# Two graph convolutions: rows as three bfloat16 parts, one-hots made by ScalarE, ring of 16 slots

## What is computed

```python
def _gcn_conv(x, src, dst, W, b):
    deg_out = jnp.maximum(jax.ops.segment_sum(ones, src, num_segments=N), 1.0)
    deg_in = jnp.maximum(jax.ops.segment_sum(ones, dst, num_segments=N), 1.0)
    h = x * (deg_out ** (-0.5))[:, None]
    h = h @ W
    m = jax.ops.segment_sum(h[src], dst, num_segments=N)
    return m * (deg_in ** (-0.5))[:, None] + b

h = _gcn_conv(layernorm(x), src, dst, W1, b1)
h = jax.nn.relu(h)
h = _gcn_conv(h, src, dst, W2, b2)
x = x + _layer_norm(h, gamma, beta)
```

## Time and profile before

| | us |
|---|---|
| median of three runs | 5920.07 |
| profiled execution, its own time | 5863.58 |
| span of the profiled execution | 5861.9 |
| TensorE busy (of the span) | 3845.1 |
| VectorE busy | 2575.1 |
| ScalarE busy | 966.5 |
| GpSimd busy | 2943.7 |
| mean granted TensorE clock | 0.793 |

### The profile page before, as it was taken

The page is one execution under the profiler, slowest core; times in us unless marked ns, Lnnn a source line. Parts: engine busy times, 40 slices in busy tenths (PEclk is TensorE's granted clock), DMA queues, the critical chain, the costliest instruction groups (busy, mean ns, idle before and its releaser), DMA issues.

```text
span 5861.9 us, 62152 instructions
## 1 busy us (share of the span) xinstructions
PE 3845.1 (66%) x14313; PEld 2804.7 (48%) x14313; DVE 2575.1 (44%) x7839; ACT 966.5 (16%) x2299; POOL 2943.7 (50%) x2860
## 2 busy tenths in 40 slices
PE   1666667777788799999355555554655555556368
PEld 0333335566667588888233333333433333334257
DVE  8433234555576511111244444445444444445841
ACT  5333232222102522222200000000200000000421
POOL 0666665565300033333366666667266666664513
PEclk9777778888898799999667767666767776767669
DMA  2333335565687344444433333332233333332202
GB/s 78 106 105 108 105 106 178 185 195 186 198 254 235 107 109 115 111 109 110 140 88 93 91 92 92 92 92 80 81 91 92 92 92 92 92 92 84 88 16 32
DMA packets 322621, 660.17 MB, mean 113 GB/s; under 512 B 60683, under 2 KB 142923, under 8 KB 322150
## 3 DMA queue, kind: packets, MB, share of 16 engines
q0 software_dynamic: 148960, 365.25, 21.4%
q1 hardware_dynamic: 152870, 253.42, 14.4%
q10 hardware_dynamic: 20448, 37.52, 2.1%
HBM read 488.94 MB, written 174.87 MB: 113 GB/s over the span
## 4 chain that ended last, share of the span: by engine, by line
PE 20%; issue 11%; DVE 10%; another core or an unknown queue 6%; DVEq 2%; DMA 1%; ACT 1%; SPq 0%; POOL 0%; POOLq 0%; ACTq 0%
PE bank L1769 15%; DVE reg_b L1313 6%; DVEq L304 2%; PE bank L1717 2%; DVE reg_a L1298 1%; PE bank L1728 1%; PE bank L1689 1%; DVEq L1313 1%; DVE small L822 0%; DVE work L1471 0%; DMA conv_rows<-work 0%; PE bank L1750 0%; DVE work L1505 0%; ACT reg_b L681 0%
## 5 line engine op out<-in xcount | busy, mean ns | idle before, releaser
L1769 PE MATMUL bank<-work,reg_a 128*128 x3520 | 1329.6, 526 | 1175.0 <-issue 626.0
L617 POOL DMA_INDIRECT work<-conv_rows,tables x1662 | 1575.8, 948 | 935.5 <-issue 482.9
L1769 PEld LDWEIGHTS bank<-work,reg_a 128*128 128x128 f32 x3520 | 821.3, 256 | 1683.2 <-issue 1570.1
L1313 DVE TENSOR_TENSOR reg_b<-reg_b,bank 128x257 f32 x1760 | 743.1, 422 | 1026.2 <-remote 518.6
L578 POOL DMA_INDIRECT messages<-work,small x880 | 884.3, 1005 | 536.3 <-ACT work L708 251.2
L1628 PE MATMUL bank<-reg_b,reg_a 128*128 x1760 | 602.8, 477 | 427.6 <-issue 191.1
L1298 DVE TENSOR_SCALAR reg_a<-iota,tables 128x128 f32<-128x128 f32 x1760 | 553.7, 315 | 274.9 <-issue 197.5
L1628 PEld LDWEIGHTS bank<-reg_b,reg_a 128*128 128x128 f32 x1760 | 363.1, 229 | 610.1 <-issue 569.8
L708 ACT ACTIVATE work<-bank,tables 128x256 f32<-128x256 f32 x880 | 397.7, 474 | 1042.5 <-PE bank L1628 630.4
L599 POOL DMA_INDIRECT residual_rows<-work,slot_t x112 | 177.9, 1589 | 478.2 <-DVE work L1282 308.3
L1641 PE MATMUL bank<-reg_b,reg_a 128*128 128x257 f32 x1544 | 395.0, 405 | 28.3 <-DVE reg_a L1164 16.3
(11 more groups left out here) (340 smaller groups left out, 3827.5 us busy)
## 6 DMA issues: line engine op xcount, KB each, us to landing
reg_b<-messages SPq DMA_DIRECT2D x316, 258.0 KB
reg_a<-in_L_ffn_W_dram SPq DMA_DIRECT2D x56, 1024.0 KB, 5.4
reg_a<-item_rows SPq DMA_DIRECT2D x110, 256.0 KB
work<-conv_rows,tables POOLq DMA_INDIRECT x1662
b_rows<-messages ACTq DMA_DIRECT2D x72, 258.0 KB
reg_b<-messages ACTq DMA_DIRECT2D x70, 258.0 KB
b_rows<-messages SPq DMA_DIRECT2D x56, 258.0 KB
messages<-work,small POOLq DMA_INDIRECT x880
```

What stands on the lines that cost most here:

```text
L617: g.indirect_dma_start(GC[:, u, 0:D], None, table, bass.IndirectOffsetOnAxis(ap=BSRC[:, b_:b_ + 1], axis=0)).then_inc(z(f"conv_in{u // 4}" ...
L1313: v.tensor_tensor(acc, acc, ps[i % 8][:, 0:D + 1], ALU.add).then_inc(z(f"{tag}_add"), 1)
L1769: pe.matmul(ps[i % 8][:, 0:D + 1], OHP[:, i % (2 * OHN), :], GCf[:, bass.ds(offs[i % 4], D + 1)], start=True, stop=True).then_inc(z(f"{tag ...
```

## The change

Each row of the tables is stored as three bfloat16 parts, head, middle and rest, whose sum is the fp32 row exactly: 768 bfloat16 values, 1536 bytes. The head is the upper half of the fp32 word; the first rest is the difference; its upper half is the middle; the second difference is the rest. ScalarE copies heads and middles, VectorE makes the two differences, chunk by chunk, in the `ln3` stage and in `c1`; the stages now write fp32 rows into a staging buffer XF (in `reg_a`) and the parts into XR.

A slot of the ring has 770 bfloat16 values, and the ring 16 slots in place of 24. TensorE makes three bfloat16 matmuls per item into the same PSUM bank with the same one-hot, the smallest part first; the column of ones stands beside the rests.

The one-hots are made by ScalarE in bfloat16, four items at a time: |iota - destination| by four Abs activations (128x128), then relu(1 - that) over 128x512, into a ring of 20 one-hots. VectorE only adds.

SyncE keeps both relays, landings and releases, in one loop (`relays`), the landings three groups ahead. The semaphores of both convolutions are shared (`conv_oh`, `conv_add`, `conv_dist`), and their counts go on from p1 to p2. The table of slot offsets is computed for the new slot count and size.

The core of the diff:

```diff
@@ setup
-    UM = UC = 24
+    UM, UC = 24, 16
-        conv1_t = dram("conv1_rows", [T * P, D])
-        conv2_t = dram("conv2_rows", [T * P, D])
+        conv1_t = dram("conv1_rows", [T * P, 3 * D], BF16)
+        conv2_t = dram("conv2_rows", [T * P, 3 * D], BF16)
-        OHN = 4
-        OHP = ta[:, 0:2 * OHN * P].rearrange("p (s n) -> p s n", n=P)
+        OHR = 20
+        OHP = ta[:, 0:OHR * P // 2].bitcast(BF16).rearrange("p (s n) -> p s n", n=P)
+        DIST = ta[:, OHR * P:(OHR + 8) * P].rearrange("p (s n) -> p s n", n=P)
-        GCf = work[:, 0:UC * (D + 1)]
-        GC = GCf.rearrange("p (u w) -> p u w", w=D + 1)
+        GCf = work[:, 0:UC * SLOT // 2].bitcast(BF16)
+        GC = GCf.rearrange("p (u w) -> p u w", w=SLOT)
+        XR = XR.bitcast(BF16).rearrange("p (s t d) -> p s t d", s=2, d=PARTS)
+        XF = ta[:, 0:2 * CH * D].rearrange("p (s t d) -> p s t d", s=2, d=D)
+        XFH = ta[:, 0:2 * CH * D].bitcast(BF16).rearrange("p (s t d k) -> p s t d k", s=2, d=D, k=2)[:, :, :, :, 1]
+        XL = B2B[:, 0:CH * D].rearrange("p (t d) -> p t d", d=D)
+        XLH = B2B[:, 0:CH * D].bitcast(BF16).rearrange("p (t d k) -> p t d k", d=D, k=2)[:, :, :, 1]
@@ SyncE
-                sp.wait_ge(*norms("ln3", "norm", c + 1))
+                for part in ("head", "middle", "rest"):
+                    sp.wait_ge(z(f"part_{part}"), PARTED["p1"] + c + 1)
                 sp.dma_start(nodes(conv1_t, c), XR[:, c % 2, :, :]).then_inc(z(f"rows_out{c % 2}"), 16)
-            def arrivals(tag):
-                for k in range(NB4):
-                    sp.wait_ge(z(f"conv_in{k % (UC // 4)}"), gathered(tag, k))
-                    sp.sem_inc(z(f"{tag}_landed"), min(4, NBLK - 4 * k))
-            arrivals("p1")
+            def arrived(tag, k):
+                sp.wait_ge(z(f"conv_in{k % (UC // 4)}"), gathered(tag, k))
+                sp.sem_inc(z(f"{tag}_landed"), min(4, NBLK - 4 * k))
+            def relays(tag):
+                for k in range(AHEAD):
+                    arrived(tag, k)
+                for k in range(NB4 - AHEAD):
+                    if k < NB4 - UC // 4:
+                        sp.wait_ge(z(f"{tag}_mm"), sp.value_load(ROW_L[:, k:k + 1], min_val=1, max_val=NI))
+                        sp.sem_inc(z(f"{tag}_free"), 4)
+                    arrived(tag, k + AHEAD)
+            relays("p1")
-                sp.wait_ge(z("relu1"), (c + 1) * CH)
+                for part in ("head", "middle", "rest"):
+                    sp.wait_ge(z(f"part_{part}"), PARTED["p2"] + c + 1)
                 sp.dma_start(nodes(conv2_t, c), XR[:, c % 2, :, :]).then_inc(z(f"rows_out{c % 2}"), 16)
-            arrivals("p2")
-            sp.wait_ge(z("p2_add"), NI)
+            relays("p2")
@@ GpSimd
-                    g.indirect_dma_start(GC[:, u, 0:D], None, table,
+                    g.indirect_dma_start(GC[:, u, 0:PARTS], None, table,
@@ ScalarE
+            def heads(tag, c):
+                if c >= 2:
+                    act.wait_ge(*parts_free(tag, c))
+                a.copy(XR[:, c % 2, :, 0:D], XFH[:, c % 2]).then_inc(z("part_head"), 1)
+            def middles(tag, c):
+                act.wait_ge(z("part_left"), PARTED[tag] + c + 1)
+                a.copy(XR[:, c % 2, :, D:2 * D], XLH).then_inc(z("part_middle"), 1)
             for c in range(NCH + 1):
                 if c < NCH:
                     ln_std("ln3", c)
                 if c >= 1:
                     if c >= 3:
-                        act.wait_ge(*rows_out((c - 1) % 2, 1, (c - 1) // 2))
-                    ln_apply("ln3", c - 1, lambda i: X[:, (c - 1) * CH + i, :], lambda i: XR[:, (c - 1) % 2, i, :])
-            def releases(tag):
-                for k in range(0, NB4 - UC // 4):
-                    act.wait_ge(z(f"{tag}_mm"), act.value_load(ROW_L[:, k:k + 1], min_val=1, max_val=NI))
-                    act.sem_inc(z(f"{tag}_free"), 4)
-            releases("p1")
+                        act.wait_ge(z("part_left"), c - 2)
+                    ln_apply("ln3", c - 1, lambda i: X[:, (c - 1) * CH + i, :], lambda i: XF[:, (c - 1) % 2, i, :])
+                    act.wait_ge(*norms("ln3", "norm", c))
+                    heads("p1", c - 1)
+                if c >= 2:
+                    middles("p1", c - 2)
+            middles("p1", NCH - 1)
+            def target_hots(tag):
+                def distances(i):
+                    if i >= 8:
+                        act.wait_ge(z("conv_oh"), CONV[tag] * NI + i - 4)
+                    for k in range(i, i + 4):
+                        ins = a.activation(DIST[:, k % 8, :], IOTA[:], ACT.Abs, bias=DREL[:, k:k + 1], scale=-1.0)
+                    ins.then_inc(z("conv_dist"), 4)
+                act.wait_ge(z("conv_ready"), CONV[tag] + 1)
+                distances(0)
+                for i in range(0, NI, 4):
+                    if i + 4 < NI:
+                        distances(i + 4)
+                    act.wait_ge(z("conv_dist"), CONV[tag] * NI + i + 4)
+                    if i >= OHR:
+                        act.wait_ge(z(f"{tag}_mm"), i - OHR + 4)
+                    a.activation(OHP[:, i % OHR:i % OHR + 4, :], DIST[:, i % 8:i % 8 + 4, :], ACT.Relu, scale=-1.0,
+                                 bias=ONES[:, 0:1]).then_inc(z("conv_oh"), 4)
+            target_hots("p1")
...
+                if c >= 1 and t % CH == 0:
+                    act.wait_ge(z("relu1"), c * CH)
+                    heads("p2", c - 1)
+                if c >= 1 and t % CH == 4:
+                    middles("p2", c - 1)
+            act.wait_ge(z("relu1"), T)
+            heads("p2", NCH - 1)
+            middles("p2", NCH - 1)
+            target_hots("p2")
@@ VectorE
-                def onehot(i):
-                    if i >= 8:
-                        v.wait_ge(z(f"{tag}_mm"), i - 7)
-                    v.tensor_scalar(OHP[:, i % 8, :], IOTA[:], DREL[:, i:i + 1], None, ALU.is_equal
-                                    ).then_inc(z(f"{tag}_oh"), 1)
-                v.memset(GC[:, :, D:D + 1], 1.0).then_inc(z(f"{tag}_one"), 1)
-                for i in range(OHN):
-                    onehot(i)
+                v.memset(GC[:, :, PARTS:PARTS + 1], 1.0).then_inc(z("conv_one"), 1)
                 for i in range(NI):
                     if i % 4 == 0:
                         offs = table_offsets(DVE_, ROW_D[:, i:i + 4], (T - 1) * (D + 1))
-                    if i + OHN < NI:
-                        onehot(i + OHN)
                     v.wait_ge(z(f"{tag}_mm"), i + 1)
                     if i:
-                        v.wait_ge(z(f"{tag}_add"), i)
+                        v.wait_ge(z("conv_add"), CONV[tag] * NI + i)
                     acc = ACCf[:, bass.ds(offs[i % 4], D + 1)]
-                    v.tensor_tensor(acc, acc, ps[i % 8][:, 0:D + 1], ALU.add).then_inc(z(f"{tag}_add"), 1)
+                    v.tensor_tensor(acc, acc, ps[i % 8][:, 0:D + 1], ALU.add).then_inc(z("conv_add"), 1)
...
+            def rests(tag, c):
+                n = PARTED[tag] + c
+                if n:
+                    v.wait_ge(z("part_middle"), n)
+                    v.wait_ge(z("part_rest"), n)
+                v.tensor_tensor(XL, XF[:, c % 2], XFH[:, c % 2], ALU.subtract).then_inc(z("part_left"), 1)
+                v.wait_ge(z("part_left"), n + 1)
+                if c >= 2:
+                    v.wait_ge(*parts_free(tag, c))
+                v.tensor_tensor(XR[:, c % 2, :, 2 * D:PARTS], XL, XLH, ALU.subtract).then_inc(z("part_rest"), 1)
+            for c in range(NCH + 2):
                 if c < NCH:
                     v.wait_ge(z(f"x_in{c}"), 16 * (2 + (c == NCH - 1)))
                     ln_stats("ln3", c, lambda i: X[:, c * CH + i, :])
-                if c >= 1:
+                if 1 <= c <= NCH:
                     ln_scale("ln3", c - 1, extra=DO)
+                if c >= 2:
+                    v.wait_ge(*norms("ln3", "norm", c - 1))
+                    rests("p1", c - 2)
...
+                c = t // CH - 1
+                if c >= 0 and t % CH == 2:
+                    v.wait_ge(z("relu1"), (c + 1) * CH)
+                    rests("p2", c)
+            v.wait_ge(z("relu1"), T)
+            rests("p2", NCH - 1)
@@ TensorE
-                            table_offsets(PE_, ROW_C[:, i:i + 4], (UC - 1) * (D + 1)))
+                            table_offsets(PE_, ROW_C[:, i:i + 4], (UC - 1) * SLOT))
                 after = places(0)
                 for i in range(NI):
                     if i % 4 == 0:
...
                         pe.wait_ge(z(f"{tag}_landed"), need)
                     if i % 4 == 1 and i + 3 < NI:
                         after = places(i + 3)
-                    pe.wait_ge(z(f"{tag}_oh"), i + 1)
+                    pe.wait_ge(z("conv_oh"), CONV[tag] * NI + i + 1)
                     if i >= 8:
-                        pe.wait_ge(z(f"{tag}_add"), i - 7)
-                    pe.matmul(ps[i % 8][:, 0:D + 1], OHP[:, i % (2 * OHN), :], GCf[:, bass.ds(offs[i % 4], D + 1)],
```

(30 more changed lines are left out.)

17 lines of the change are left out of this document (11 added, 6 removed).

## The result

The changed kernel takes 6022.3 us (median; 6020.1 to 6025.0) against 5919.9 (5917.0 to 5927.4): ratio 1.0177, interval 1.016 to 1.0194, 102 us slower. The forecast was 5969, 49 slower. The sign and the range held; the forecast was less than half of the measured size.

A forecast was written before the change was run, and what follows sets the result against it. No engine is full; POOL's pauses over its 1.2525 us per gather, from cycles with a slow half, bound the convolutions. Loops +28, edges +20, +29, -22, -6 give +49: 5863.6 + 49 + 56.5 = 5969 us, range 5625 to 6190.

The forecast's parts named there:

- The loops: Gather loops of both convolutions: slightly slower pace of TensorE and VectorE, +14 us each, +28 for two (0 to +120).
- the balance: Formula for POOL's streak in a loop cycle, pause 3.2 us, fast half 10.5 us: rate 1.417 to 1.434 us a gather.
- f: Time per item in the fast half of a loop cycle: 0.75 us before, 0.80 taken for the change.
- s: Time per item in the slow half of a loop cycle: 3.1 us before, 3.3 taken, 4.1 as bound.
- S: Gathers in one POOL streak between pauses, by formula: 19.5 before, 17.6 taken for the change.
- Before conv1: Splitting rows in the statistics stage: VectorE becomes the pace at 8.3 us per chunk, +20 us (10 to 35).
- Before conv2: Splitting rows in the linear stage: 3 us per chunk, 21, plus 8 after the last Relu, +29 us (8 to 62).
- End of conv1: No VectorE one-hot held beside POOL's pass over X, -22 us (-24 to 0); fewer items left, -3.
- B: Rival for the loops: slow halves vanish, POOL streams at its floor, 5639 us; chance 0.28 with its partial form.
- A: The forecast itself: pause cycle stays, edges cost, a gather every 1.43 to 1.46 us, 5969 us; chance 0.41.
- C: Rival for the loops: TensorE's item sets the pace, streaks of 8 to 12, +86 per convolution, 6113 us; chance 0.24.
- D: Rival for the loops: pauses follow bytes or packets, which grow by half, +76 per convolution, 6093 us; chance 0.05.

The follow-up runs named there:

- before_again: The kernel before, unaltered, run for a second profile where POOL never pauses: 5301.7 us.
- after_short_rows: Changed kernel with tables and gathers of two of three parts (1024 bytes), still three matmuls, where POOL never pauses: 5355.9 us, ratio 1.0102.
- fp32_act_hots: Kernel before with one-hots on ScalarE and relays on SyncE, fp32 rows and ring of 24 kept, where POOL never pauses: 5293.4 us, ratio 0.9985.
- the second set: Runs where POOL pauses, kernel before at 5915.3 us: changed kernel unaltered 6020.0; kernel before with a ring of 16, 5904.3.
- the fifth: Set where POOL pauses, kernel before at 5877.4 us: changed kernel with two-part tables 5979.6, unaltered 5983.4; kernel before with ring of 16, 5861.5.
- narrow_fp32: Kernel before with ScalarE's one-hots, SyncE's relays and ring of 16, its fp32 product cut to 96 of 257 columns: 5855.4 us beside 5868.0.
- fp32_act_hots_c: Kernel before with ScalarE's one-hots and SyncE's relays, fp32 and ring of 24, rerun where POOL pauses: 5852.2 us, ratio 0.9963.

## Why the prediction was right or wrong

**What bounds the kernel** was read rightly: pauses of POOL over a floor of 1.2525, in cycles with a slow stretch. In the changed kernel such a stretch looks so:

```profile
3388.00 0.42 DVE L1372 TENSOR_TENSOR reg_b<-reg_b,bank 128x257 f32 x1 [0.20 <-DVE reg_b L1372]
...
3390.60 0.42 DVE L1372 TENSOR_TENSOR reg_b<-reg_b,bank 128x257 f32 x1 [2.18 <-PE bank L1851]
...
3393.36 0.35 PE L1851 MATMUL bank<-work,reg_a 128*128 x1 [0.43 <-issue]
...
3394.15 0.42 DVE L1372 TENSOR_TENSOR reg_b<-reg_b,bank 128x257 f32 x1 [3.12 <-PE bank L1851]
...
3395.95 0.42 DVE L1372 TENSOR_TENSOR reg_b<-reg_b,bank 128x257 f32 x1 [0.20 <-DVE reg_b L1372]
```

Adds mostly 0.62 us apart until 3388.0, then 2.6 and 3.6 us apart, then 0.62 again; PE's matmuls single between.

The prediction says that no view names what slows PE. The trace does show it, in the rows of PE's sequencer (PEldq), which don't count as busy. Below is its register step ahead of the product (count: ns min/median/max), in this order: the fast half of the cycle of the earlier trace rows, the slow half, the slow stretch above in the changed kernel, and before_again, where POOL never pauses:

```profile
L1769 PEldq FUSED_REGOPS  x11: 37/37/37, 3397.1 to 3405.6; - x11
...
L1769 PEldq FUSED_REGOPS  x5: 10/685/700, 3407.5 to 3419.3; - x5
...
L1851 PEldq FUSED_REGOPS  x6: 3/695/700, 3388.3 to 3394.0; - x6
...
L1769 PEldq FUSED_REGOPS  x420: 37/37/37, 3000.9 to 3498.9; - x140
```

The same step takes 37 ns in one half and some 700 in the other. PE's sequencer has 330 and 300 steps of 0.60 to 0.76 us in the two convolutions of before, 391 and 390 in those of after, 2 and 3 in before_again and none in after_short_rows. VectorE's sequencer has none in before and after: there VectorE waits for PE. Why a step takes 0.7 us stays open. The sets show that it belongs to where the kernel runs and not to the kernel (two chips without pauses, three others with; the two chips that came twice kept their kind, though one of them had before at 5915 and at 5873): the same program has it or not, the message stage with it (1394 to 1438 us with pauses, 1155 to 1160 without). I had taken the pause as a property of the loop.

**POOL's cost per gather, SyncE's relays, ScalarE's one-hots, the shorter ring at 0**: right. 945 ns with 1536 bytes; relays 5300.8 against 5301.0; 0.50 us an item where 0.69 was the bound; ring of 16 at 1.436. The rule of the Trainium skill ("ScalarE: Activation LUTs", Rules for kernel authors) to use VectorE for simple functions agrees with the trace in direction: a one-hot costs 0.50 us on ScalarE against 0.315 on VectorE. The kernel is none the slower for it (fp32_act_hots: 0.9985), since neither engine sets the end.

**The loops: the step that failed.** +14 each was taken; +28 was measured in the second set (1230.5 and 1230.1 us against 1202.9 and 1201.5), +30 in the fifth (1224.5 and 1220.8 against 1193.0 and 1192.1), 42 between the first two profiles. The step that failed is the balance: it kept the fast half of a cycle at 10.5 us and the pause at 3.2, and let the change act on the pace alone (f 0.80 for 0.75, s 3.3 for 3.1). The adds of the two profiles show what happened. Call a stretch fast where at least five adds in a row start within 1.6 us of the one before, and the rest slow; both convolutions together:

| | before | after |
|---|---|---|
| fast stretches: mean length, us an item | 10.5, 0.81 | 6.2, 0.84 |
| slow stretches: mean length, us an item | 11.6, 3.8 | 7.4, 3.3 |
| items in fast and in slow stretches | 1391, 326 | 1333, 398 |
| time in fast and in slow stretches, us | 1124, 1236 | 1114, 1329 |

f moved little, as taken. s fell, where a rise was taken. What changed is the length of a fast stretch, 6.2 us in place of 10.5, and with it the number of items that fall into slow ones. The whole loss of the loops stands in slow stretches, and other limits than 1.6 us (1.4, 2.0) show the same. The bound f = 0.94, s = 4.1 gave 1.49, near the 1.486 of the profile, but with S = 13.5 and values of f and s that didn't come: that it fits is luck.

The formula also lets TensorE's pace set the streaks. With one matmul in place of three the streaks grew from 8 to 20 and the pauses from 2.1 to 4.2, and the rate went from 1.472 to 1.4655 only. Of 0.036 the number of matmuls owns 0.007 (across two sets, before at 5873 and 5877), the bytes 0.004, and the rest, 0.025, if the shares add up, came with the bfloat16 form of the product: all four kernels with it have 1.463 to 1.486, all five with the fp32 form 1.434 to 1.447. What in the form does it is open. It is not the clock alone (narrow_fp32), not the ring, not ScalarE's making the one-hots, not SyncE. That slot sizes, the type of the one-hots or the weight loads (123 ns each on the mean in place of 256) play a part wasn't tried. Nor does the number of slow steps decide it: fp32_act_hots_c has 404 and 450 of them on PE and runs at 1.434.

**Before conv1**, +20 taken, +25 measured. VectorE's subtractions, ScalarE's copies were sized rightly (2.02 for 2.04, 1.68 for 1.8), but a chunk takes 8.5 us and more:

```profile
2903.75 2.02 DVE L1482 TENSOR_TENSOR b_rows<-reg_a 128x1792 f32<-128x1792 f32 x1 [0.58 <-ACT work L807]
...
2908.92 1.68 ACT L802 COPY work<-reg_a 128x1792 bf16<-128x1792 bf16 x1 [1.62 <-DMA conv_rows<-work]
...
2912.28 2.03 DVE L1482 TENSOR_TENSOR b_rows<-reg_a 128x1792 f32<-128x1792 f32 x1 [0.25 <-ACT work L807]
...
2947.35 1.03 POOL L649 DMA_INDIRECT work<-conv_rows,tables  x1 [66.69 <-DMA conv_rows<-work]
```

8.53 from one first subtraction to the next, since the subtraction waits for the copy of the middle before it (L807), and that for the write of two chunks earlier (L802 idles 1.62 us behind the DMA). A chain through both engines and the write was costed as VectorE's own sum.

**Before conv2**, +29 taken, +44 measured (from the end of the degrees, 70.6 to 114.9). The chain of a chunk:

```profile
4251.70 1.67 ACT L802 COPY work<-reg_a 128x1792 bf16<-128x1792 bf16 x1
...
4255.33 2.02 DVE L1482 TENSOR_TENSOR b_rows<-reg_a 128x1792 f32<-128x1792 f32 x1
...
4257.38 2.03 DVE L1486 TENSOR_TENSOR work<-b_rows 128x1792 bf16<-128x1792 f32 x1
...
4260.66 2.08 PE L1769 MATMUL bank<-reg_b,work 128*128 128x256 f32 x4 [3.03 <-ACT work L779]
4260.91 1.67 ACT L807 COPY work<-b_rows 128x1792 bf16<-128x1792 bf16 x1
...
4266.60 1.67 ACT L802 COPY work<-reg_a 128x1792 bf16<-128x1792 bf16 x1
```

ScalarE's head (1.67), VectorE's two subtractions (4.05) and ScalarE's middle (1.67) each stand in the middle of the linear stage's own work, and TensorE waits 3.03 us behind them. A chunk takes 14.9 us (4251.70 to 4266.60) in place of 9.5. I put 3 between 0 and 7.7 as if half would hide; 5.6 of 7.7 did not (105.3 against 66.3 us up to the last Relu). Behind the last Relu 5.2 stood where 8 was taken.

**End of conv1**, -22 and -3 taken, -15 measured:

```profile
4181.97 24.51 POOL L675 TENSOR_TENSOR reg_a<-reg_a,reg_b 128x12544 f32<-128x12544 f32 x1
4182.30 0.42 DVE L1372 TENSOR_TENSOR reg_b<-reg_b,bank 128x257 f32 x1 [2.46 <-PE bank L1851]
...
4183.74 0.42 DVE L1372 TENSOR_TENSOR reg_b<-reg_b,bank 128x257 f32 x1 [1.02 <-remote]
...
4193.36 13.19 DVE L1504 TENSOR_SCALAR small<-reg_b 128x49 f32<-128x49 f32 x1
```

The adds do run beside POOL's pass of 24.5 us, as I said. But the first instruction behind them that has both operands in SBUF, the degrees (L1504, 0.20 us before), is held for 13.19. The stall was moved behind the loop, not removed; what is next was not asked. **End of conv2**: -3 taken, -6 measured.

In sum the loops came to 56 to 60 where 28 stood and the edges to 46 to 50 where 21 stood; both were doubled: the loops by a balance that held the wrong thing fixed, the edges by terms between two far bounds that were put near the cheap one (3 us a chunk before conv2, and nothing for the next instruction behind the stall).

**The rivals.** B had its case in other sets: no pauses, 1.251. It had nothing to do with the change, though. A's own sign, a gather every 1.43 to 1.46, did not come either (1.472 to 1.486), and C's streaks of 8 did. C's value of 1.538 was not reached, since its pause of 3.2 did not stay: in the commonest streaks pauses shrink with streaks, as A has it (8 with 2.0 after, 16 with 3.2 before, 20 with 4.2 with one matmul). C's sum also takes its +86 from the seen 1.434, where A's +14 starts from the formula's 1.417; from there it would be +100. D fell (0.004 of 0.036).

## What to carry to other kernels

When work is moved into a stage "between" other work, cost the chain of one chunk through all engines, and take a value near the serial bound unless a row shows the slack. When a stall is removed, look for the next instruction of the same kind behind it. When a formula balances two stretches of a cycle, ask whether their lengths stay as they are, and look at the steps of an engine's sequencer where its busy rows show only gaps. And take a second profile, if there is one, before a rate's second decimal carries a sum: here the profile of before was 56 us under its own median.
